# A short product ahead of the first projection, two buffers for the head products, and a new order of slots on all engines

## The chip, the cores and the metric

The kernel runs on one core of a Trainium2 chip. The metric is the time of one execution on the device in microseconds (us), launch to end; lower is better. All data are 32-bit floats, but for small mask matrices in bf16. A 32-bit product shows in the trace as two matmul records.

## What is computed

A gated cross-attention block followed by a gated feed-forward block, on x of shape (32, 56, 128). The context has 1500 rows for each batch item, but the causal mask lets 56 queries see only its first 56 rows.

```python
def xattn(Q, K, V):                       # 16 heads of 64
    q, k, v = heads(Q @ Wq), heads(K @ Wk), heads(V @ Wv)
    attn = softmax(where(causal, q @ k.T / 8, -1e9))
    return merge(attn @ v) @ Wo
def ffn(x):
    h = rmsnorm(x, gamma1)
    q = h @ Wq + bq                        # each token: 16 heads of 8
    k, v = split((h @ Wdown + bdown) @ Wup + bup)
    att = softmax(einsum('bthd,btgd->bthg', q, k) / sqrt(8))   # heads against heads, inside one token
    x = x + einsum('bthg,btgd->bthd', att, v) @ Wo + bo
    h2 = rmsnorm(x, gamma2)
    gate = softmax(h2 @ Wg + bg)           # 8 experts, all of them computed
    return x + einsum('btd,edf,bte->btf', h2, We, gate)
x = x + tanh(g_xattn) * xattn(layernorm(x), ctx, ctx)
x = x + tanh(g_ffn) * ffn(layernorm(x))
```

## The kernel before, in words

The five engines each run one instruction queue, written out by hand; the order of the calls in each block is the order of execution, and semaphores join the queues. There is no planner.

The attention works in 16 steps t of two batch items (T = 112 tokens). The feed-forward works in 14 tiles f of 128 tokens, with the stages of three or four successive tiles side by side in a step: in the loops, `fa` is the tile that enters in step t, `fb` the one that entered a step earlier, `fc` two and `fd` three steps earlier. Tile 9 is fa in step 12, tile 10 in step 13, tile 11 in step 14, tile 12 in step 15; tile 13 enters behind the last step. Lines 1065 to 1117 are TensorE's loops, 519 to 566 ScalarE's, 771 to 817 VectorE's, 359 to 384 GpSimd's; each engine has one loop for t = 2 to 13, one for t = 14 and 15, and then a list written out for the end, for tiles `third` = 11, `prior` = 12, `last` = 13. Steps 2 to 13 also hold the projection of queries or keys for later steps (`project`, PROJECT_AT); steps 14 and 15 hold none.

On TensorE a step is: `scores(t)`, `new_y(t-1)` (output projection of the attention), `turn_o` (transposes the head outputs of tile fc), `shift(t)` (subtracts the row maxima in PSUM), `bias_o`, `new_o`, the projections, `turn_x2`, two `values`, `turn_probs(t)`, `gate_logits`, `first(fa)` (transposes the new residual and makes q, k, v of the tile), `attend(t)`, two `expert_half`. A warm-up product of the identity (line 850) runs before the first key projection.

VectorE (DVE): `score_max` (L610), `products` (L642: part of the products query x key, for heads against heads), `new_x1` (L628), `logits` (L647: a reduction of 2048 products a row), `new_x2` (L685), `prob_sums` (L615), `norm` (L619, L622), `shifted_logits`, `weighted` (L661, L665), `gate_logits` (L691), `head_sums` (L674, again 2048 a row), `gate_sum`, `scaled_qkv` (L633), `head_scales` (L669), `normed_heads` (L680). GpSimd (POOL) makes the other heads' share of both kinds of product (L310, L318) and normalizes most of the probabilities (L300), sums the experts (L324 to L332), and does powers (L338, L342) and the gate (L347). ScalarE (ACT) copies PSUM out, takes exponentials (L430, L458, L478), `kv_copy` (L454: copies keys and values of the tile into PSUM, from where DVE's products read them), `squares` (L469, L470), `x2_copy` (L474) and the eight `experts` copies (L485).

`prod1` (query x key) and `prod2` (weight x value) are one buffer each, 8 KB a partition. Whoever writes a tile's products waits until the sums of the tile before are made. For tile 12 alone (PE_SUMS) TensorE makes both sums, by products with the identity (L994, L1001), and for tiles 10 to 12 (PE_OUT) it also adds the ten terms of the output (`output_sums`), which ScalarE copies out (`late_out`). The tail is what follows step 15: the serial chain of tiles 11, 12 and 13.

Of the kernel before, what the change touches and what calls it, by code (L numbers as in the profile page):

```python
# [14 lines left out]
D = 128  # L15
NP = 16
# [7 lines left out]
FH = 16  # L24
FD = 8
E = 8
L = 64
HP = 10
HQ = 6
# [12 lines left out]
def product_heads(f):  # L42
    return (HP_LATE, HQ_LATE) if f >= LATE else (HP, HQ)

# [10 lines left out]
LATE = 10  # L55
HP_LATE = 8
HQ_LATE = 5
PE_SUMS = (12,)
# [43 lines left out]
def build(nc, xp, x_t, ctx_t, wq, wk, wv, wo, fw, fup, fdn, fwe, out):  # L102
    with ExitStack() as stack:
# [66 lines left out]
        prod1 = sb("prod1", [128, FH, FH, FD])  # L170
        prod2 = sb("prod2", [128, FH, FD, FH])
# [42 lines left out]
        prod1_d = prod1[:, :, :, :].rearrange("p a b c -> p (a b c)").rearrange("p (d h g) -> p d h g", d=FD, h=FH)  # L214
        prod2_g = prod2[:, :, :, :].rearrange("p a b c -> p (a b c)").rearrange("p (g h d) -> p g h d", g=FH, h=FH)

        def logit_products(f, lo, hi, k, q):
            n = hi - lo
            if f in PE_SUMS:
                return (prod1_d[:, :, lo:hi, :],  # L220
                        k.rearrange("p (g d) -> p d g", g=FH).unsqueeze(2).to_broadcast([128, FD, n, FH]),
                        q.rearrange("p (h d) -> p d h", h=n).unsqueeze(3).to_broadcast([128, FD, n, FH]))
            return (prod1[:, lo:hi, :, :],
# [3 lines left out]
        def head_products(f, lo, hi, v):  # L227
            n = hi - lo
            if f in PE_SUMS:
                return (prod2_g[:, :, lo:hi, :],  # L230
                        e_sb[f % 2][:, lo:hi, :].rearrange("p h g -> p g h").unsqueeze(3).to_broadcast([128, FH, n, FD]),
                        v.rearrange("p (d g) -> p g d", d=FD).unsqueeze(2).to_broadcast([128, FH, n, FD]))
            return (prod2[:, lo:hi, :, :],
# [38 lines left out]
        def _(pool):  # L272
# [39 lines left out]
            def weighted(f):  # L312
                pool.wait_ge(s["e_ready"], f + 1)
                if f > 0:
                    pool.wait_ge(s["oraw_ready"], f)
# [84 lines left out]
        def _(act):  # L400
# [118 lines left out]
            for t in range(2, TAIL):  # L519
# [7 lines left out]
                if fc is not None:  # L527
                    squares(fc)
                    x2_copy(fc)
# [658 lines left out]
```

## Time and profile before

| | before |
|---|---|
| median of 3 runs | 265.05 us (264.35 to 265.61) |
| the profiled execution | 265.27 us, span 263.3 us |
| VectorE, ScalarE, GpSimd busy | 73%, 65%, 57% of the span |
| chain that ended last, by engine | PE 60%, DVE 17%, POOL 8%, issue 7%, ACT 5% |
| DMA, mean over the span | 28 GB/s, nearly all of it in the first tenth |

The span runs from the first to the last instruction of the profiled execution. Busy time is an average over stages with different limits: what an edit is worth is read where it lies, from what TensorE and the others wait for there.

### The profile page before, as it was taken

How to read it: one execution, taken by the hardware profiler on the slowest of the kernel's cores; microseconds unless marked ns; L12 is line 12 of the kernel's file. 1: busy time of each engine (PE TensorE's matmuls, PEld its weight loads, DVE VectorE, ACT ScalarE, POOL GpSimd, SP SyncE). 2: the span in 40 equal slices, each digit the busy share in tenths (PEclk: the TensorE clock that was granted, in tenths of full speed). 3: DMA queues.
4: the chain of work that ended last, by engine and by line, in shares of the span. 5: the costliest groups of instructions: out<-in, count | busy, mean ns of one | idle time of the engine just before them, and what ended most of it. 6: DMA issues, size and time to landing. Idle time of an engine off the chain costs nothing.

```text
span 263.3 us, 7886 instructions
## 1 busy us (share of the span) xinstructions
PE 246.5 (94%) x3242; PEld 177.4 (67%) x3242; DVE 192.0 (73%) x333; ACT 170.8 (65%) x501; POOL 149.8 (57%) x157
## 2 busy tenths in 40 slices
PE   5989989997989999999999999999899999988995
PEld 2775778675858676777678585867586656467664
DVE  0136744088989888898989751889898799968944
ACT  2437534756586877787787768675778676852273
POOL 4103030346468788787878473864796879656220
PEclk9999999999999999999999999999999999999999
DMA  6990000000000000000000000000000000000000
GB/s 211 365 311 9 2 4 0 5 1 2 2 2 0 12 4 10 4 10 5 11 2 12 2 11 2 0 15 0 2 2 10 4 14 4 10 2 0 10 2 30
DMA packets 6017, 7.30 MB, mean 28 GB/s; under 512 B 477, under 2 KB 4830, under 8 KB 5982
## 3 DMA queue, kind: packets, MB, share of 16 engines
q1 hardware_dynamic: 5550, 6.16, 7.3%
q8 instruction: 26, 0.43, 0.7%
q10 hardware_dynamic: 432, 0.64, 0.7%
q14 instruction: 9, 0.07, 0.1%
HBM read 5.88 MB, written 0.92 MB: 26 GB/s over the span
## 4 chain that ended last, share of the span: by engine, by line
PE 60%; DVE 17%; POOL 8%; issue 7%; ACT 5%; DMA 1%; POOLq 0%; SPq 0%; DVEq 0%
PE ps_a L853 34%; PE ps_c L853 9%; PE ps_b L853 7%; PE ps_e L853 6%; POOL prod L310 4%; PE ps_b L905 4%; DVE ps_e L674 3%; DVE ps_e L647 3%; POOL prod L318 2%; DVE psums L615 2%; DMA cT<-in_ctx_t 1%; DVE prod L665 1%; ACT probs L430 1%; POOL probs L300 1%; DVE fqkv L633 1%
## 5 line engine op out<-in xcount | busy, mean ns | idle before, releaser
L300 POOL TENSOR_TENSOR probs<-probs,prinv 120x672 f32<-120x672 f32 x16 | 24.3, 1517 | 38.5 <-DVE prinv L619 38.4
L310 POOL TENSOR_TENSOR prod<-fqkv 128x1280 f32<-128x1280 f32 (+1 forms) x14 | 38.7, 2762 | 5.5 <-DVE fqkv L633 2.7
L853 PE MATMUL ps_a<-aT,wo_sb 128*128 128x112 f32 x256 | 32.8, 281 | 0.6 <-ACT aT L424 0.3
L853 PEld LDWEIGHTS ps_a<-aT,wo_sb 128*128 128x128 f32 x256 | 29.9, 191 | 3.3 <-ACT aT L424 1.5
L853 PE MATMUL ps_a<-wv_sb,cT 128*64 128x512 f32 x128 | 31.4, 606 | 0.0
L647 DVE TENSOR_REDUCE ps_e<-prod 128x256 f32<-128x2048 f32 x13 | 29.7, 2285 | 1.8 <-POOL prod L310 1.8
L674 DVE TENSOR_REDUCE ps_e<-prod 128x128 f32<-128x2048 f32 x13 | 29.7, 2287 | 1.7 <-POOL prod L318 1.6
L853 PE MATMUL ps_a<-cT,wk_sb 128*128 128x224 f32 x128 | 29.4, 384 | 1.4 <-DMA cT<-in_ctx_t 1.4
L485 ACT ACTIVATE exb<-ps_c,gate 128x128 f32<-128x128 f32 x88 | 25.0, 386 | 6.2 <-POOL gate L347 6.2
L853 PEld LDWEIGHTS ps_a<-cT,wk_sb 128*128 128x128 f32 x128 | 24.9, 206 | 5.9 <-DMA cT<-in_ctx_t 3.0
L318 POOL TENSOR_TENSOR prod<-e_sb,fqkv 128x768 f32<-128x768 f32 (+1 forms) x14 | 24.5, 1752 | 6.2 <-PE ps_e L853 3.6
L853 PE MATMUL ps_a<-xT,wqc 128*128 128x224 f32 x128 | 27.0, 359 | 0.6 <-ACT qT L413 0.6
L413 ACT COPY kT<-ps_a 128x448 f32<-128x448 f32 x32 | 17.0, 532 | 13.7 <-PE ps_a L853 13.4
L610 DVE TENSOR_REDUCE nmax<-ps_b 120x16 bf16<-120x896 f32 x15 | 16.3, 1089 | 12.5 <-PE ps_b L853 12.5
L853 PEld LDWEIGHTS ps_a<-xT,wqc 128*128 128x128 f32 x128 | 22.7, 190 | 3.9 <-ACT qT L413 2.4
L853 PEld LDWEIGHTS ps_a<-probsT,v_sb 56*64 56x64 f32 x1024 | 16.5, 134 | 9.3 <-issue 5.7
L413 ACT COPY qT<-ps_a 128x448 f32<-128x448 f32 x32 | 16.9, 533 | 8.8 <-PE ps_a L853 8.7
L853 PE MATMUL ps_c<-fwe_sb,x2T 128*128 128x512 f32 x44 | 22.4, 623 | 0.1
L905 PEld LDWEIGHTS ps_b<-ident,probs 120*128 120x128 f32 x120 | 12.2, 140 | 14.7 <-issue 14.7
L419 ACT COPY v_sb<-ps_a 128x512 f32<-128x512 f32 x32 | 17.9, 589 | 5.4 <-PE ps_a L853 5.4
L665 DVE TENSOR_TENSOR prod<-e_sb,ps_e 128x1280 f32<-128x1280 f32 (+1 forms) x14 | 21.2, 1515 | 0.0
L430 ACT ACTIVATE probs<-ps_b,rstd 120x896 f32<-120x896 f32 x15 | 15.1, 1008 | 8.5 <-PE ps_b L853 7.5
(144 smaller groups left out, 487.7 us busy)
## 6 DMA issues: line engine op xcount, KB each, us to landing
xp_sb<-in_xp SPq DMA_DIRECT2D x1, 896.0 KB, 7.9
out<-out_sb SPq DMA_DIRECT2D x14, 64.0 KB, 1.5
xT<-in_x_t SPq DMA_DIRECT2D x1, 784.0 KB, 9.1
cT<-in_ctx_t SPq DMA_DIRECT2D x1, 784.0 KB, 10.7
wv_sb<-in_wv SPq DMA_DIRECT2D x1, 512.0 KB, 7.6
wo_sb<-in_wo SPq DMA_DIRECT2D x1, 512.0 KB, 12.3
fwe_sb<-in_fwe SPq DMA_DIRECT2D x1, 512.0 KB, 8.9
fw_sb<-in_fw SPq DMA_DIRECT2D x1, 266.0 KB, 12.2
```

Source lines behind the costliest of these rows:

```text
L300: nc.gpsimd.tensor_tensor(pr[0:TG, NC:C, :, 0:S], pr[0:TG, NC:C, :, 0:S], prinv[p % 2][0:TG, NC:C, :].unsqueeze(3).to_broadcast([TG, C - N ...
L310: nc.gpsimd.tensor_tensor(o, k, q, ALU.mult).then_inc(s["prod1_pool"], 1)
L318: nc.gpsimd.tensor_tensor(o, e, v, ALU.mult).then_inc(s["prod2_pool"], 1)
L413: nc.scalar.copy(dst[:, 2 * k:2 * k + 2, :], ps_a[:, b, 0:2 * GT].rearrange("p (c t) -> p c t", c=2)).then_inc(a_free[b], 1)
L419: nc.scalar.copy(v_sb[p % 2][:, bt, :, :], ps_a[:, b, :].rearrange("p (c d) -> p c d", c=C)).then_inc(a_free[b], 1)
L430: nc.scalar.activation(probs[p % 2][0:TG, :, :, 0:S].rearrange("p c r k -> p r c k"), score_banks(p)[0:TG, :, 0:C * S].rearrange("p r (c k ...
L485: last = nc.scalar.activation(exb[f % XB][:, e, :], expert_banks(f)[:, half, e % 4 * D:(e % 4 + 1) * D], ACT.Copy, scale=gate[f % 2][:, e: ...
L647: nc.vector.tensor_reduce(ps_e[:, f % 2, 0:2 * D].rearrange("p (h g) -> p h g", h=FH), prod1[:, :, :, :], AX.X, ALU.add).then_inc(s["logit ...
L665: nc.vector.tensor_tensor(o, e, v, ALU.mult).then_inc(s["prod2_ready"], 1)
L674: nc.vector.tensor_reduce(ps_e[:, f % 2, 0:D].rearrange("p (h d) -> p h d", h=FH), prod2[:, :, :, :], AX.X, ALU.add).then_inc(s["oraw_read ...
L853: return nc.tensor.matmul(o, lhsT, rhs, start=start, stop=stop, skip_group_check=True)
L905: ins = nc.tensor.transpose(score_banks(p)[:, ch // 4, ch % 4 * 128:ch % 4 * 128 + TG], probs[p % 2][0:TG, ch, :, :].rearrange("p r k -> p ...
```

## The change

It does four things.

1. The warm-up of one product of 512 columns becomes two, of 512 and of 384 columns.
2. `prod1` and `prod2` get two buffers each, by the tile's parity, so that writers wait for the sums of the tile two before. The count of sums becomes a function (`sums_made`), and the heads that TensorE sums a table (`LOGITS_BY_PE`, `HEADS_BY_PE`); their values, 16 heads for tile 12, keep the split as it was. So does POOL_HEADS (8 and 5 heads for tiles 10 to 13).
3. Steps 2 to 13: ScalarE has `x2_copy` ahead of `squares`, the first `attended` ahead of `gate_exps`, `kv_copy` ahead of the experts; DVE has `head_scales` right behind `weighted`; TensorE makes the second expert half first.
4. Steps 14 and 15 and the tail get a new order on TensorE, ScalarE, DVE and GpSimd.

```diff
-PE_SUMS = (12,)
+LOGITS_BY_PE = {12: 16}
+HEADS_BY_PE = {12: 16}
...
-        prod1 = sb("prod1", [128, FH, FH, FD])
-        prod2 = sb("prod2", [128, FH, FD, FH])
+        prod1 = two("prod1", [128, FH * FH * FD])
+        prod2 = two("prod2", [128, FH * FD * FH])
...
             def products(f):                                    # GpSimd; weighted(f) likewise
                 pool.wait_ge(s["qkv_ready"], f + 1)
-                if f > 0:
-                    pool.wait_ge(s["logit_ready"], f)
+                if f >= 2:
+                    pool.wait_ge(s["logit_ready"], sums_made(LOGITS_BY_PE, f - 2))
...
@@ GpSimd, steps 14 and 15, then the tail
                 outputs(fd)
+                second_scale(fc)
                 norm(t)
-                second_scale(fc)
...
             products(prior)
             first_scale(last)
+            second_scale(third)
             products(last)
             weighted(prior)
-            second_scale(third)
+            gating(third)
             weighted(last)
-            gating(third)
             second_scale(prior)
+            gating(prior)
             last_residual(last)
-            gating(prior)
             second_scale(last)
@@ ScalarE, steps 2 to 13
                 if fc is not None:
+                    x2_copy(fc)
                     squares(fc)
-                    x2_copy(fc)
...
+                if t < NP:
+                    attended(t, 0)
                 if fc is not None:
                     gate_exps(fc)
                 if t < NP:
-                    attended(t, 0)
                     attended(t, 1)
-                if fc is not None:
-                    experts(fc, 0)
                 if fa is not None:
                     kv_copy(fa)
                 if fc is not None:
+                    experts(fc, 0)
                     experts(fc, 1)
@@ ScalarE, steps 14 and 15
                 exps(t)
+                squares(fc)
+                values(t, 0)
                 x2_copy(fc)
-                values(t, 0)
-                squares(fc)
                 x1_copy(fa)
+                head_exps(fb)
                 values(t, 1)
+                gate_exps(fc)
                 turned_probs(t)
-                gate_exps(fc)
-                head_exps(fb)
+                kv_copy(fa)
                 attended(t, 0)
                 attended(t, 1)
-                kv_copy(fa)
+                experts(fc, 0)
                 experts(fc, 1)
-                experts(fc, 0)
@@ DVE, steps 14 and 15
+                products(fb)
                 score_max(t)
-                products(fb)
+                logits(fb)
                 new_x1(t - 1)
                 new_x2(fc)
                 prob_sums(t)
                 norm(t)
-                logits(fb)
+                shifted_logits(fb)
                 gate_logits(fc)
-                shifted_logits(fb)
+                weighted(fb)
                 scaled_qkv(fa)
                 gate_sum(fc)
-                weighted(fb)
                 head_scales(fb)
                 head_sums(fb)
@@ TensorE, the warm-up
-            nc.tensor.matmul(ps_b[:, 0, :], ident[:, :], ident[:, :].unsqueeze(1).to_broadcast([128, 4, 128]), start=True, stop=True)
+            for n in (4, 3):
+                nc.tensor.matmul(ps_b[:, 0, 0:n * 128], ident[:, :], ident[:, :].unsqueeze(1).to_broadcast([128, n, 128]), start=True, stop=True)
@@ TensorE, steps 14 and 15
                 shift(t)
+                values(t, 0)
                 bias_o(fc)
                 new_o(fc)
-                values(t, 0)
                 turn_x2(fc)
                 first(fa)
+                gate_logits(fc)
                 values(t, 1)
-                gate_logits(fc)
                 turn_probs(t)
```

The lists of the tail, as they stand after the change:

```python
# TensorE: last, prior, third = 13, 12, 11
new_y(15); turn_o(third); bias_o(third); new_o(third); first(last); logit_sums(prior)
output_sums(10); turn_x2(third); gate_logits(third); expert_half(third, 0); head_sums(prior)
expert_half(third, 1); turn_o(prior); bias_o(prior); new_o(prior); turn_x2(prior)
output_sums(third); gate_logits(prior); turn_o(last); bias_o(last); new_o(last)
expert_half(prior, 1); turn_x2(last); expert_half(prior, 0); gate_logits(last)
expert_half(last, 1); expert_half(last, 0); output_sums(prior)
# ScalarE
o_copy(third); x1_copy(last); squares(third); kv_copy(last); head_exps(prior); x2_copy(third)
gate_exps(third); head_exps(last); experts(third, 0); o_copy(prior); experts(third, 1)
squares(prior); x2_copy(prior); o_copy(last); late_out(10); late_out(third); gate_exps(prior)
squares(last); x2_copy(last); experts(prior, 1); experts(prior, 0); gate_exps(last)
experts(last, 0); late_out(prior)
# DVE, up to where it is as before
products(prior); new_x1(15); new_x2(third); scaled_qkv(last); shifted_logits(prior)
products(last); weighted(prior); gate_logits(third); head_scales(prior); logits(last)
shifted_logits(last); gate_sum(third); normed_heads(prior); weighted(last); new_x2(prior)
head_scales(last); head_sums(last); normed_heads(last)
```

## Rows read from the trace of the kernel before

**Rows 1.** The page: TensorE's share of busy time, its granted clock in 40 slices.
```profile
PE 246.5 (94%) x3242; PEld 177.4 (67%) x3242; DVE 192.0 (73%) x333; ACT 170.8 (65%) x501; POOL 149.8 (57%) x157
...
PEclk9999999999999999999999999999999999999999
```

**Rows 2.** Timeline of TensorE from the start: start us, length us, engine, line, operation.
```profile
1.56 2.08 PE L850 MATMUL ps_b<-ident 128*128 128x512 f32 x2 [1.56 <-POOL ident L276]
5.02 5.87 PE L853 MATMUL ps_a<-cT,wk_sb 128*128 128x224 f32 x16 [1.39 <-DMA cT<-in_ctx_t]
10.73 1.88 PE L853 MATMUL ps_e<-wq_sb,cmat 128*128 128x512 f32 x4
```

**Rows 3.** Timeline of ScalarE: its copies behind the key and the query projection.
```profile
8.42 0.53 ACT L413 COPY kT<-ps_a 128x448 f32<-128x448 f32 x1 [0.96 <-PE ps_a L853]
9.91 0.53 ACT L413 COPY kT<-ps_a 128x448 f32<-128x448 f32 x1 [0.96 <-PE ps_a L853]
10.93 0.53 ACT L413 COPY kT<-ps_a 128x448 f32<-128x448 f32 x1 [0.49 <-PE ps_a L853]
...
13.51 0.53 ACT L413 COPY qT<-ps_a 128x448 f32<-128x448 f32 x1 [1.13 <-PE ps_a L853]
14.26 0.53 ACT L413 COPY qT<-ps_a 128x448 f32<-128x448 f32 x1 [0.22 <-PE ps_a L853]
```

**Rows 4.** The query weights: the issue in the timeline, and the landing by DMA.
```profile
1.64 0.46 ACTq L403 DMA_DIRECT2D wq_sb<-in_wq  x1
...
wq_sb<-in_wq ACTq DMA_DIRECT2D x1, 256.0 KB, 4.9
```

**Rows 5.** Stretches: length; busy of PE, PEld, DVE, ACT, POOL; clock; DMA share; GB/s.
```profile
104.00:118.00 14.00, 14.00 (x199) 10.06 (x197) 12.45 (x20) 11.03 (x35) 10.99 (x12) 1.00 0.02 6
```

**Rows 6.** Timeline of all engines, step 14.
```profile
205.62 2.36 POOL L310 TENSOR_TENSOR prod<-fqkv 128x1024 f32<-128x1024 f32 x1
...
206.52 0.40 ACT L454 COPY ps_e<-fqkv 128x256 f32<-128x256 f32 x1
...
206.76 1.09 DVE L610 TENSOR_REDUCE nmax<-ps_b 120x16 bf16<-120x896 f32 x1 [0.67 <-PE ps_b L853]
207.77 1.21 DVE L642 TENSOR_TENSOR prod<-ps_e,fqkv 128x1024 f32<-128x1024 f32 x1
...
209.64 0.35 DVE L685 SCALAR_TENSOR_TENSOR x<-xc,rstd,ps_c 128x128 f32<-128x128 f32 x1 [0.42 <-PE ps_c L853]
...
210.22 1.09 DVE L615 TENSOR_REDUCE psums<-probs 120x16 f32<-120x896 f32 x1 [0.23 <-ACT probs L430]
...
211.67 1.52 POOL L300 TENSOR_TENSOR probs<-probs,prinv 120x672 f32<-120x672 f32 x1
...
211.94 2.29 DVE L647 TENSOR_REDUCE ps_e<-prod 128x256 f32<-128x2048 f32 x1
...
213.34 1.01 PE L905 MATMUL ps_b<-ident,probs 120*128 120x120 f32 x8 [0.38 <-POOL probs L300]
```

**Rows 7.** Timeline: the last output projection of the attention, behind step 15.
```profile
230.60 2.04 PE L853 MATMUL ps_a<-aT,wo_sb 128*128 128x112 f32 x16
```

**Rows 8.** Timeline of all engines in the tail, in order of time.
```profile
238.66 2.37 POOL L310 TENSOR_TENSOR prod<-fqkv 128x1024 f32<-128x1024 f32 x1 [1.79 <-PE ps_e L853]
...
242.85 3.81 PE L853 MATMUL ps_e<-prod,ident 128*128 128x128 f32 x32 [0.30 <-POOL prod L318]
...
253.07 0.35 DVE L685 SCALAR_TENSOR_TENSOR x<-xc,rstd,ps_c 128x128 f32<-128x128 f32 x1 [0.94 <-PE ps_c L853]
...
253.84 2.40 PE L853 MATMUL ps_e<-exb,ident 128*128 128x128 f32 x20
...
255.29 2.18 ACT L485 ACTIVATE exb<-ps_a,gate 128x128 f32<-128x128 f32 x8 [0.74 <-POOL gate L347]
...
256.07 0.29 PE L853 MATMUL ps_c<-fwg_sb,x2T 128*128 128x8 f32 x2
...
257.30 0.32 ACT L478 ACTIVATE ps_c<-glog,gmax 128x8 f32<-128x8 f32 x1
```

More of the change, by code:

```diff
@@ L42, in product_heads, with sums_made @@
 def product_heads(f):
-    return (HP_LATE, HQ_LATE) if f >= LATE else (HP, HQ)
+    return POOL_HEADS.get(f, (HP, HQ))
+def sums_made(by_pe, f):
+    return sum((by_pe.get(n, 0) > 0) + (by_pe.get(n, 0) < FH) for n in range(f + 1))
 def first_step(f):
@@ L212, in expert_banks, with logit_tiles, head_tiles @@
             return {"a": ps_a, "b": ps_b}[BIG[f]] if f in BIG else ps_c
[L214 to L215 removed]
+        def logit_tiles(f):
+            n, t = LOGITS_BY_PE.get(f, 0), prod1[f % 2]
+            return (t[:, 0:n * FH * FD].rearrange("p (d h g) -> p d h g", d=FD, h=n) if n else None,
+                    t[:, n * FH * FD:].rearrange("p (h g d) -> p h g d", g=FH, d=FD) if n < FH else None)
+        def head_tiles(f):
+            n, t = HEADS_BY_PE.get(f, 0), prod2[f % 2]
+            return (t[:, 0:n * FH * FD].rearrange("p (g h d) -> p g h d", g=FH, h=n) if n else None,
+                    t[:, n * FH * FD:].rearrange("p (h d g) -> p h d g", d=FD, g=FH) if n < FH else None)
         def logit_products(f, lo, hi, k, q):
[L218 to L220 removed]
+            n, by_pe, (tp, td) = hi - lo, LOGITS_BY_PE.get(f, 0), logit_tiles(f)
+            if hi <= by_pe:
+                return (tp[:, :, lo:hi, :],
                         k.rearrange("p (g d) -> p d g", g=FH).unsqueeze(2).to_broadcast([128, FD, n, FH]),
                         q.rearrange("p (h d) -> p d h", h=n).unsqueeze(3).to_broadcast([128, FD, n, FH]))
[L223 removed]
+            return (td[:, lo - by_pe:hi - by_pe, :, :],
                     k.rearrange("p (g d) -> p g d", g=FH).unsqueeze(1).to_broadcast([128, n, FH, FD]),
@@ L553, in _ @@
                 exps(t)
+                squares(fc)
+                values(t, 0)
                 x2_copy(fc)
-                values(t, 0)
-                squares(fc)
                 x1_copy(fa)
+                head_exps(fb)
                 values(t, 1)
+                gate_exps(fc)
                 turned_probs(t)
-                gate_exps(fc)
-                head_exps(fb)
+                kv_copy(fa)
                 attended(t, 0)
                 attended(t, 1)
-                kv_copy(fa)
+                experts(fc, 0)
                 experts(fc, 1)
-                experts(fc, 0)
             last, prior, third = NT - 1, NT - 2, NT - 3
+            o_copy(third)
             x1_copy(last)
-            o_copy(third)
+            squares(third)
+            kv_copy(last)
             head_exps(prior)
-            kv_copy(last)
-            squares(third)
             x2_copy(third)
+            gate_exps(third)
             head_exps(last)
-            late_out(PE_OUT[0])
-            o_copy(prior)
-            gate_exps(third)
-            x2_copy(prior)
-            squares(prior)
-            experts(third, 1)
-            o_copy(last)
-            experts(third, 0)
+            experts(third, 0)
+            o_copy(prior)
+            experts(third, 1)
+            squares(prior)
+            x2_copy(prior)
+            o_copy(last)
+            late_out(PE_OUT[0])
+            late_out(third)
             gate_exps(prior)
@@ L589, in _ @@
             gate_exps(last)
-            late_out(third)
             experts(last, 0)
@@ L819, in _ @@
             last, prior, third = NT - 1, NT - 2, NT - 3
+            products(prior)
             new_x1(NP - 1)
-            products(prior)
+            new_x2(third)
             scaled_qkv(last)
             shifted_logits(prior)
-            new_x2(third)
+            products(last)
             weighted(prior)
-            products(last)
+            gate_logits(third)
             head_scales(prior)
@@ L829, in _ @@
             shifted_logits(last)
-            gate_logits(third)
+            gate_sum(third)
             normed_heads(prior)
@@ L834, in _ @@
             head_scales(last)
-            gate_sum(third)
             head_sums(last)
@@ L1120, in _ @@
             new_y(NP - 1)
+            turn_o(third)
             bias_o(third)
+            new_o(third)
             first(last)
             logit_sums(prior)
-            turn_o(third)
-            new_o(third)
             output_sums(PE_OUT[0])
@@ L1128, in _ @@
             gate_logits(third)
+            expert_half(third, 0)
             head_sums(prior)
+            expert_half(third, 1)
+            turn_o(prior)
             bias_o(prior)
-            turn_o(prior)
             new_o(prior)
-            expert_half(third, 1)
             turn_x2(prior)
-            expert_half(third, 0)
+            output_sums(third)
             gate_logits(prior)
-            expert_half(prior, 0)
             turn_o(last)
@@ L1142, in _ @@
             turn_x2(last)
-            output_sums(third)
+            expert_half(prior, 0)
             gate_logits(last)
```

56 lines of the change are left out of this document (31 added, 25 removed).

## Prediction

> **What bounds the kernel now.** I read the page's shares first, then the engine's own waits, then the timeline where those waits lie. TensorE (PE) is busy for 94% of the span [rows 1], and in the middle of the run (one step per two batch items) the table of stretches shows it busy without a hole, VectorE (DVE) and GpSimd (POOL) having air [rows 5]. A new order of the other engines' work is worth nothing there, as long as it makes nobody later than TensorE. So the change can only act where TensorE waits or runs slowly: the first 12 us, the two last attention steps, and the 31 us behind them, where the last three feed-forward tiles pass serially over all engines.
>
> The start: the granted clock reads 9 tenths from the first slice on [rows 1], but the durations disagree. ScalarE's copies behind the key projection follow each other by 1.49 us for four matmul records, those behind the query projection by 0.75 us [rows 3]. The same records take exactly twice as long: 1.2 GHz against 2.4 GHz. Between the third and the fourth key copy lie 1.02 us; with 0.373 a record slow and 0.187 fast, 1.02 = 0.373n + 0.187(4 - n) gives n = 1.5, so the clock rose at 5.02 + 13.5 x 0.373 = 10.05 us, 5.0 us after the projections began. The product on the identity that runs before them, 1.56 to 3.64, is followed by 1.4 us of idleness [rows 2] and brought nothing.
>
> **The warm-up.** One product of 512 columns (two records, 2.08 us) becomes two, of 512 and 384. At the slow rate a record of 224 columns takes 0.373, so one of 512 takes 0.85 and one of 384 takes 0.64. Four records end at 1.56 + 2 x 0.85 + 2 x 0.64 + 0.2 of drain = 4.75 us, before the keys' input lands at 5.02: nothing is queued behind them that could have run earlier, with 0.27 us to spare; if the input came at once, they would cost that much. TensorE is then occupied from 1.56 with a hole of only 0.27 us instead of 1.4. Before, the rise came 5.0 us after unbroken work began; counted from 1.56 it falls at 6.6. Then 4.2 records run slowly and 9.2 records that were slow run fast, at 0.19 saved each: **-1.7 us**. The bounds: nothing (the hole counts as a new start) and -2.5 (fast from 5.02 on: 13.5 x 0.187). I take 1.7, since it moves a measured distance. Next behind it are transfers: the weights of the queries, issued at 1.64, landed 4.9 later at 6.5 [rows 4]; they were used at 10.73 [rows 2] and would be at 9.0. The rest of the front is a chain of TensorE, ScalarE and DVE, which moves as a whole.
>
> The Trainium skill ("TensorE: Matmul & The Clock Gate", Part 1) says that the low level is the default which activity releases, and that the moment differs from run to run. It also says the ramp costs under 1% of a typical span: an estimate by that sentence caps this term at 2.6 us, just above my -2.5. Its statement on runs makes my 1.7 a mean that single runs miss; that is the first rival below.
>
> **Steps 2 to 13.** On ScalarE the copy of x2T goes ahead of the squares, and the copy of the feed-forward keys and values (kv_copy) ahead of the eight expert copies; one DVE reciprocal comes forward, the expert halves change places. Each exchange moves a result by one or two instructions of 0.2 to 1 us under a TensorE that is full [rows 5]: 0, bounds -0.2 and +0.2 over all. The double buffers of the head products bring nothing here either: POOL's products wait for this tile's qkv, which comes long after the previous tile's sums.
>
> **Steps 14 and 15.** Here DVE gets a new order: products of the heads before the score maximum, and the long reduction (logits, 2.29 us) before new_x1, new_x2 and the sums of the probabilities, on which POOL's normalization and TensorE's transposes hang. Step 14 walked along, in the times of before: qkv is there at about 205.6, when POOL's products start. kv_copy no longer waits for four expert copies and starts then instead of at 206.52; DVE's products run 206.05 to 207.2 (1.21, overlapping the next), the maximum to 208.2 (score products end at 206.7), the reduction needs POOL's products, which end at 205.62 + 2.36 = 207.98, and takes DVE to 210.4; x1 and x2 at about 0.3 each, and the sums start at 210.9 against 210.22. POOL's normalization moves by the same, 211.67 to 212.33, ends at 213.85, and the transposes go from 213.34 to 213.98, **+0.64** [rows 6]. TensorE gives part of it back: the expert product now follows the transposes with its input ready, where it had waited for the gate logits, so the step ends +0.4. In exchange the reduction after the normalization (211.94) is gone, and the tile's output is 1.2 us earlier in front of step 15. There DVE starts its queue 1.2 us sooner, pays 2.2 for the reduction and ends at +0.8 at the transposes, +0.55 at the last attention output (before: 230.60 [rows 7]). Bounds: 0 and +4.4, two whole reductions.
>
> **The tail.** The +0.55 is mostly swallowed at once: TensorE's logit sums of tile 12 had waited for DVE's product and not for TensorE's own queue, and the walk has them beginning only 0.1 later. From there on: (1) POOL's products of tile 13 start at 238.66, 1.79 after they could, because the one buffer was being summed [rows 8]. With two buffers their qkv decides, 237.9. So POOL's second product of tile 12 ends 0.7 earlier, and the head sums on TensorE, at 242.85 before, start when DVE is done, 242.55: **-0.3**. This -0.3 persists through the second reduction to tile 13's x2, 253.07 to 252.8. (2) The output sums of tile 11 (20 records, 2.4 us) stood between the transposition of tile 13's x2 and its gate logits, 253.84 to 256.07. They move ahead, into the wait for tile 13's head output. What is late next? The row scale r2, which needs squares (0.5), POOL's residual and power (0.5 each): 254.9, and ScalarE, which after x2T has the eight expert copies of tile 12 before tile 13's gate exponentials. They take 257.30 - 255.29 = 2.0 us. They had waited for a gate at 255.29; the new order has gate and products ready when ScalarE finishes x2T, at 252.8 + 1.2 = 254.0. The gate exponentials then start at 254.0 + 2.05 = 256.05 instead of 257.30: **-1.25**, the -0.3 included. From there to the end everything is as before, 6.0 us. Bounds: -0.3 (the sums merely change places with another wait) and -2.2 (all of the 2.4 us, less what the next engine adds).
>
> **The sum.** 265.27 (the profiled execution; its span 263.3 and 2.0 around it) - 1.7 - 1.25 = 262.3. That execution lies 0.2 above the median 265.05, so the prediction is **262.1**, with 261.2 to 263.0 as the likeliest case's own range (0.3 for the clock, 0.5 for the walk).
>
> **The rivals.**
> - The warm-up moves nothing: the clock keeps its own schedule or takes the hole for a new start. For it: 2.08 us of activity in front brought nothing so far, and the hole remains. Against it: the hole shrinks from 1.4 to 0.27. Time 265.05 - 1.25 = 263.8. Chance 0.12. By the Trainium skill's sentence on differences from run to run (same page, Part 1) it would be so in some executions only; no trace here shows more than one start.
> - The tail gives its gain back: the moved output sums now stand before tile 13's transposition of the head output (my walk has 0.2 us between them), or ScalarE's late copies push the exponentials. Then 265.05 - 1.7 - 0.3 = 263.1. Chance 0.13.
> - Both gain more: an early rise (-2.5) and DVE in steps 14 and 15 covered by TensorE: 260.7. Chance 0.08.
> - Slower: the long reduction ahead of the probability sums. If DVE's earlier start does not absorb it, each of steps 14 and 15 is 2.2 longer, 4.4 in place of the 0.55 of my walk: 262.1 + 3.85 = 266.0. The kernel is slower than before once the two steps lose more than 0.55 + 2.95 = 3.5 together. For it: in step 14 only 0.2 us lie between POOL's last product (207.98) and DVE's readiness (208.2), so every delay of POOL passes on [rows 6]. Against it: kv_copy is 0.9 earlier, and in step 15 the room is 2 us. Chance 0.07, a little over half of it past the 266.4 that would count as slower.
> - My forecast: 0.60.
>
> **How the numbers follow.** About 0.5%, 1.3 us, can be told from no change here, so faster means under 263.7. That is all of the forecast and of the third rival, and most of the second: 0.60 + 0.08 + 0.09 = 0.77. Same takes the first rival (0.12) and the rest of the second and the fourth (0.04 and 0.03): 0.19. Slower 0.04. The range goes from 260.7 to 263.9, which leaves out the slower case, and the edges of the others.
>
> **What would show it.** Key copies on ScalarE 0.75 us apart from the second or third on, and the query weights' product at about 9.0 instead of 10.73; nothing waits for a transfer. Steps of 14.1 us in the middle as before. In step 14 the transposes 0.6 us later against the start of the step, the reduction before the sums. In the tail, POOL's products of tile 13 begin before TensorE's logit sums end; the gate exponentials of the last tile 24.9 us after the last attention output projection begins, against 26.7 before (257.30 - 230.60). Wrong would be: the fourth key copy still 1.0 us or more after the third with the product at 10.7; new holes of over 1 us in steps 14 and 15 whose releaser is x2; or the last gate logits again waiting on TensorE.

## The result, and the profile after

The changed kernel takes 262.34 us (median of 4 runs, 260.77 to 262.57); the kernel before took 265.31 on the same chip (264.35 to 265.61). The ratio is 0.9882, with an interval of 0.9835 to 0.9928. In a later set of runs it was 261.74 against 265.05, 0.9885 (0.9866 to 0.9904). Predicted were 262.1, 260.7 to 263.9. The profiled execution took 262.38, with a span of 260.3; that of before had 263.3.

The page, answering to [rows 1]: busy times, the granted clock, and the chain that ended last by engine.

```profile
PE 245.8 (94%) x3244; PEld 177.2 (68%) x3244; DVE 190.3 (73%) x333; ACT 171.4 (66%) x501; POOL 150.1 (58%) x157
...
PEclk9999999999999999999999999999999999999999
...
PE 67%; DVE 19%; POOL 6%; ACT 6%; issue 2%; DVEq 0%; POOLq 0%; ACTq 0%
```

Busy times moved by under 2 us each. In the chain the share of "issue" went from 7% to 2%, but that is no measure of the gain: it would be 13 us, and another execution of the same changed kernel (a_again, below) has 4%. Where the 3.0 us lie has to be read from the timelines. First TensorE's start, answering to [rows 2], and ScalarE's key copies, answering to [rows 3].

```profile
1.56 3.35 PE L868 MATMUL ps_b<-ident 128*128 128x512 f32 x4 [1.56 <-POOL ident L289]
4.93 4.67 PE L871 MATMUL ps_a<-cT,wk_sb 128*128 128x224 f32 x16
9.44 1.88 PE L871 MATMUL ps_e<-wq_sb,cmat 128*128 128x512 f32 x4
```

```profile
6.83 0.53 ACT L426 COPY kT<-ps_a 128x448 f32<-128x448 f32 x1 [3.22 <-PE ps_a L871]
8.00 0.53 ACT L426 COPY kT<-ps_a 128x448 f32<-128x448 f32 x1 [0.63 <-PE ps_a L871]
8.76 0.53 ACT L426 COPY kT<-ps_a 128x448 f32<-128x448 f32 x1 [0.23 <-PE ps_a L871]
```

The warm-up ends at 4.91 and the projection follows at 4.93, without the hole. The first two copies are 1.17 apart and the next two 0.76: by the equation of the prediction 1.17 is 2.3 slow records and 1.7 fast ones, so the clock rose at 4.93 + 6.3 x 0.373 = 7.3 (predicted 6.6, before 10.05). The query weights' product starts at 9.44 (predicted 9.0, before 10.73).

The last 20 us, answering to [rows 8], first on TensorE.

```profile
245.98 0.39 PE L871 MATMUL ps_c<-fw_sb,ident 128*128 128x128 f32 x2
246.75 0.49 PE L871 MATMUL ps_c<-fw_sb,oT 128*128 128x128 f32 x2 [0.39 <-ACT oT L476]
247.68 0.33 PE L984 MATMUL ps_c<-ident,x 128*128 128x128 f32 x1 [0.44 <-DVE x L702]
247.85 2.47 PE L871 MATMUL ps_e<-exb,ident 128*128 128x128 f32 x20
250.15 0.29 PE L871 MATMUL ps_c<-fwg_sb,x2T 128*128 128x8 f32 x2
250.32 0.33 PE L967 MATMUL ps_c<-ident,onorm 128*128 128x128 f32 x1
...
252.20 0.27 PE L984 MATMUL ps_c<-ident,x 128*128 128x128 f32 x1
...
253.17 0.28 PE L871 MATMUL ps_c<-fwg_sb,x2T 128*128 128x8 f32 x2
```

The output sums (20 records, 2.47 us) now run between the transpositions of tile 12's x2 and tile 13's head output, where TensorE would wait. Behind the transposition of tile 13's x2 (252.20) the gate logits come 0.97 later; before, with the sums in between, it was 2.34 (253.73 to 256.07). Next, ScalarE's and DVE's last instructions: gate exponentials and last output.

```profile
252.67 2.18 ACT L498 ACTIVATE exb<-ps_a,gate 128x128 f32<-128x128 f32 x8
254.68 0.33 ACT L491 ACTIVATE ps_c<-glog,gmax 128x8 f32<-128x8 f32 x1
...
257.54 0.27 ACT L505 COPY out_sb<-ps_e 128x128 f32<-128x128 f32 x1 [0.71 <-PE ps_e L871]
```

```profile
258.00 0.29 DVE L743 TENSOR_TENSOR out_sb<-exb 128x128 f32<-128x128 f32 x1
```

The exponentials start when ScalarE is through the eight expert copies, 24.55 us after the last attention output projection (230.13); before it was 26.70.

All runs below are read in the same segments. The columns: the start of the query weights' product; the length of step 14, from its first score products to those of step 15, and of step 15, from there to the last output projection; from the last output projection to the gate exponentials of tile 13; from those to the end of the span; the span. The times stand beside before on the same chip. Left out of the ratios are one execution of e4_no_hole (347.46 us, mean granted clock 0.659; it is its only trace, so it has no row here) and one of before (348.51 us).

| run | product | step 14 | step 15 | to the exponentials | to the end | span | median | before | ratio (interval) |
|---|---|---|---|---|---|---|---|---|---|
| before | 10.73 | 12.13 | 13.00 | 26.70 | 6.00 | 263.3 | | | |
| changed | 9.44 | 12.68 | 13.03 | 24.55 | 5.62 | 260.3 | 262.34 | 265.31 | 0.9882 (0.9835, 0.9928) |
| a_again, the same | 8.86 | 12.68 | 13.31 | 24.56 | 5.67 | 259.8 | 261.74 | 265.05 | 0.9885 (0.9866, 0.9904) |
| e1_warm_only | 8.34 | 12.12 | 13.00 | 26.68 | 6.03 | 260.9 | 263.15 | 264.87 | 0.9947 (0.9927, 0.9967) |
| e2_no_warm | 10.20 | 12.67 | 13.02 | 24.54 | 5.62 | 260.8 | 262.65 | 264.87 | 0.9925 (0.9904, 0.9947) |
| e3_no_product | 9.77 | 12.12 | 12.99 | 26.70 | 5.99 | 261.9 | 264.40 | 264.87 | 0.9988 (0.9971, 1.0004) |
| e5_one_buffer | 8.25 | 12.67 | 13.02 | 24.89 | 5.66 | 259.8 | 261.87 | 264.73 | 0.9902 (0.9874, 0.9930) |
| e6_two_buffers | 10.36 | 12.13 | 12.99 | 26.48 | 7.60 | 264.3 | 265.21 | 264.73 | 1.0018 (0.9997, 1.0039) |
| e7_old_steps | 8.87 | 12.12 | 13.00 | 25.91 | 5.62 | 260.5 | 262.39 | 264.73 | 0.9920 (0.9893, 0.9947) |
| e8_sums_late | 9.43 | 12.68 | 13.23 | 28.80 | 6.37 | 265.2 | 265.95 | 264.73 | 1.0059 (1.0030, 1.0088) |
| e9_filler | 8.53 | 12.68 | 13.02 | 26.06 | 6.36 | 261.9 | 264.47 | 265.05 | 0.9982 (0.9958, 1.0007) |
| e11_split | 8.75 | 12.13 | 14.68 | 24.56 | 5.66 | 260.5 | 262.75 | 265.05 | 0.9932 (0.9903, 0.9962) |
| e12_split_early | 8.39 | 12.13 | 14.69 | 24.55 | 5.64 | 260.6 | 262.94 | 265.05 | 0.9939 (0.9917, 0.9962) |

What the table leaves out hardly differs: from the product to the scores of step 2 28.62 us (29.22 in e5_one_buffer), steps 3 to 13 154.2 in all. Only step 2 has between 11.48 and 12.42, mostly by a pause of TensorE in its output projection, of at most 0.70 us (0.42 in the changed kernel, 0.20 before), for which the profile names no releaser ("issue"), and which goes with no edit (step 2 took 12.15 and 11.88 in two executions of the changed kernel). Such pauses, of 0.60 and 0.52 us, also stand in step 15 of a_again (13.31) and e8_sums_late (13.23). So the change's 3.0 us of span are: front -1.29, step 2 +0.22, steps 14 and 15 +0.58, up to the exponentials -2.15, from there to the end -0.38.

### The profile page after: what moved, and what is told of

Read it like the earlier page. It is cut to its first block, busy times and chain, and to the rows that moved or that the text cites. A ratio compares the mean times of both kernels' runs of the same rounds, so it can differ in the third digit from the quotient of the medians.

```text
span 260.3 us, 7887 instructions
## 1 busy us (share of the span) xinstructions
PE 245.8 (94%) x3244; PEld 177.2 (68%) x3244; DVE 190.3 (73%) x333; ACT 171.4 (66%) x501; POOL 150.1 (58%) x157
## 4 chain that ended last, share of the span: by engine, by line
PE 67%; DVE 19%; POOL 6%; ACT 6%; issue 2%; DVEq 0%; POOLq 0%; ACTq 0%
PE ps_a L871 35%; PE ps_c L871 10%; PE ps_e L871 7%; PE ps_b L871 7%; DVE ps_e L662 4%; PE ps_b L923 4%; POOL prod L323 3%; DVE ps_e L691 2%; DVE psums L628 2%; DVE prod L680 2%; POOL probs L313 2%; ACT exb L498 2%; PE ps_b L868 1%; DVE fqkv L646 1%; DVE nmax L623 1%
## 5 line engine op out<-in xcount | busy, mean ns | idle before, releaser
L871 PE MATMUL ps_a<-cT,wk_sb 128*128 128x224 f32 x128 | 28.2, 372 | 0.0
L871 PEld LDWEIGHTS ps_a<-cT,wk_sb 128*128 128x128 f32 x128 | 23.7, 198 | 4.0 <-ACT kT L426 1.9
L498 ACT ACTIVATE exb<-ps_c,gate 128x128 f32<-128x128 f32 x88 | 23.9, 381 | 1.1 <-POOL gate L360 0.8
L437 ACT COPY aT<-ps_a 128x448 f32<-128x448 f32 x32 | 16.3, 531 | 6.2 <-PE ps_a L871 6.0
## 6 DMA issues: line engine op xcount, KB each, us to landing
fw_sb<-in_fw SPq DMA_DIRECT2D x1, 266.0 KB, 11.9
```

The lines of the kernel that those rows point to most:

```text
L498: last = nc.scalar.activation(exb[f % XB][:, e, :], expert_banks(f)[:, half, e % 4 * D:(e % 4 + 1) * D], ACT.Copy, scale=gate[f % 2][:, e: ...
L871: return nc.tensor.matmul(o, lhsT, rhs, start=start, stop=stop, skip_group_check=True)
```

## The experiments

**The warm-up by itself, and the rest by itself.** e1_warm_only is the kernel before with this edit alone; e2_no_warm the changed kernel with the opposite edit.

```diff
-            nc.tensor.matmul(ps_b[:, 0, :], ident[:, :], ident[:, :].unsqueeze(1).to_broadcast([128, 4, 128]), start=True, stop=True)
+            for n in (4, 3):
+                nc.tensor.matmul(ps_b[:, 0, 0:n * 128], ident[:, :], ident[:, :].unsqueeze(1).to_broadcast([128, n, 128]), start=True, stop=True)
```

> The kernel before with only the two warm-up products (512 and 384 columns) in place of one. Theory (the rise of TensorE's clock moves forward with the start of nearly unbroken work): the product of the query weights starts near 9.4 us as in the changed kernel, 1.3 us earlier than before, all later stages keep their lengths, and the time is 1.3 us below the kernel before, 264.0. Rival (the clock keeps its own schedule and the changed kernel's trace was one lucky phase): the product starts near 10.7 and the time is that of before, 265.3.

> The changed kernel with the single old warm-up product. Theory: the front returns to the old one (query weights near 10.7), everything behind keeps the changed lengths, 262.3 + 1.3 = 263.6, so 1.7 below the kernel before by the new order alone. Rival (the new order brought it all, the clock nothing on the mean): 262.3.

The ratio 0.9947 on 264.87 is -1.4 us (0.9 to 1.9); 0.9925 is -2.0 (1.4 to 2.5). The two make 3.4 together, within their intervals the -3.05 of the same kernel in a_again. Both parts gain; by these figures the new order gains more, though the two intervals overlap. Expected were 1.3 and 1.7. e1_warm_only's start on TensorE:

```profile
1.56 3.31 PE L851 MATMUL ps_b<-ident 128*128 128x512 f32 x4 [1.56 <-POOL ident L276]
5.02 3.49 PE L854 MATMUL ps_a<-cT,wk_sb 128*128 128x224 f32 x16
```

The same 16 records took 5.87 us before [rows 2], 4.67 in the changed kernel and 3.49 here, all fast from the first. So what the warm-up brings differs from one execution to the next.

**How little, and how much, warm-up.** e3_no_product is the kernel before without its product; e4_no_hole has `for n in (4, 3, 1)`, which ends behind the landing of the keys' input; e12_split_early (below) has products from a tile of ones that DVE writes first, `for n in (4, 4, 1)`, so that they begin at 1.04 and not at 1.56.

> The kernel before without any product ahead of the first projection (it is not part of the result). Theory (the old product, followed by 1.4 us of idleness, bought nothing): 265.3 and query weights near 10.7, as before. Rival (any activity in front helps a little): up to 0.8 us slower, the key copies 1.49 us apart up to the last one.

> The kernel before with three products ahead, of 512, 384 and 128 columns, so that they end at the moment the keys' input lands and the hole of some 0.1 to 0.3 us closes. Theory (the small hole costs nothing): as with two products, 264.0, query weights near 9.4. Rival (the hole still delays the rise): the rise comes earlier by up to 1.5 us and the time is 263.3 to 263.5. If the third product is in the way of the keys, they start up to 0.2 later.

Without any product the query weights' product starts at 9.77, and the ratio is 0.9988 (0.9971 to 1.0004): the one product of before was worth nothing that can be measured. e4_no_hole took 263.66 against 264.87, 0.9952 (0.9935 to 0.9968), like e1_warm_only: closing the last hole adds nothing that can be measured. Over the traces of the table, the one with three products (e12_split_early, 8.39) left out, with one product or none the start was at 10.73, 10.20, 10.36 and 9.77 (mean 10.27), with two at 9.44, 8.34, 8.25, 8.87, 9.43, 8.86, 8.53 and 8.75 (mean 8.81): **-1.46**, and the two groups do not overlap.

The moment of the rise moves between executions with the same first 5 us. The Trainium skill ("TensorE: Matmul & The Clock Gate", Part 1) says so too, and here the traces agree: the query weights' product starts at 8.86 and 9.44 in two executions of one and the same kernel.

**The buffers.** e5_one_buffer is the changed kernel with one buffer, e6_two_buffers the kernel before with two (and the waits of DVE for PE_SUMS dropped, which the second buffer makes needless).

```diff
-        prod1 = two("prod1", [128, FH * FH * FD])
-        prod2 = two("prod2", [128, FH * FD * FH])
+        prod1 = [sb("prod1", [128, FH * FH * FD])] * 2
+        prod2 = [sb("prod2", [128, FH * FD * FH])] * 2
...
-                if f >= 2:
-                    pool.wait_ge(s["logit_ready"], sums_made(LOGITS_BY_PE, f - 2))
+                if f >= 1:
+                    pool.wait_ge(s["logit_ready"], sums_made(LOGITS_BY_PE, f - 1))
```

> The changed kernel with one buffer again for each kind of head product, and the waits that go with it; all orders as changed. Theory (POOL's products of tile 13 then wait for TensorE's logit sums of tile 12, near 237.4 instead of 236.9, and the second kind for the head sums): 0.5 to 1.0 us slower than the changed kernel, 262.9 to 263.3. Rival (the buffers carry most of the tail's gain): 1.5 or more slower, 263.8 and above. Rival (the order carries all): 262.3.

> The kernel before with only the second buffers and their relaxed waits, no order changed, no longer warm-up. Theory (in the old order DVE's product and then TensorE's own queue follow): POOL's products of tile 13 start 0.8 earlier (near 237.9), the head sums 0.2 to 0.3 earlier, the last gate logits remain behind the output sums: 265.1, within 0.3 of before. Rival (the buffers are the gain of the tail): 1 us or more below before, under 264.3.

POOL's products of tile 13 in e5_one_buffer:

```profile
236.65 2.36 POOL L323 TENSOR_TENSOR prod<-fqkv 128x1024 f32<-128x1024 f32 x1 [0.84 <-PE ps_e L871]
```

They wait 0.84 for TensorE's sums; in the changed kernel they wait for qkv alone (236.89, 0.20). The exponentials come 24.89 after the last output projection and not 24.55: the buffers are worth 0.34 in the new order and 0.22 in the old (26.70 against 26.48). Neither can be seen in a time: 0.9902 has 0.9885 in its interval, and 1.0018 has 1. For e5_one_buffer I had expected a loss of 0.5 to 1.0, which was too much, and 262.9 to 263.3, which its early front (product at 8.25) put further off; the segment is what answers the question. The profiled execution of e6_two_buffers ends 1.6 later than that of before, counted from the exponentials: its last two output transfers landed 3.4 and 3.2 us after their issue, against 1.5 and 1.6 before. Why they did stays open.

**The order of steps 14 and 15.** e7_old_steps is the changed kernel with the loops `for t in range(TAIL, END)` of before on all four engines; warm-up, buffers and the lists of the tail stay new.

> The changed kernel with the old order in steps 14 and 15 on all four engines; warm-up, buffers and the new tail stay. Theory (the new order costs 0.55 in the two steps, and the tail swallows most of it): the last attention output starts 0.55 earlier than in the changed kernel, the tail is longer by as much, 262.3 within 0.3. Rival (what the steps lose is lost): 261.8. Rival (the new order of the steps is what makes the new tail fast, by earlier outputs of tile 11): 263 or more.

The steps are back at 12.12 and 13.00, 0.59 less, but the tail takes 25.91 instead of 24.55. DVE around the last output projection (228.97 in this run), e7_old_steps:

```profile
229.15 2.25 DVE L691 TENSOR_REDUCE ps_e<-prod 128x128 f32<-128x2048 f32 x1
231.43 0.29 DVE L697 TENSOR_TENSOR onorm<-ps_e,einv 128x128 f32<-128x128 f32 x1
231.64 1.21 DVE L655 TENSOR_TENSOR prod<-ps_e,fqkv 128x1024 f32<-128x1024 f32 x1
232.77 0.32 DVE L641 SCALAR_TENSOR_TENSOR x1T<-ps_a,gates,xT 128x112 f32<-128x112 f32 x1
```

The changed kernel (projection at 230.13):

```profile
228.66 2.23 DVE L691 TENSOR_REDUCE ps_e<-prod 128x128 f32<-128x2048 f32 x1
230.93 0.29 DVE L697 TENSOR_TENSOR onorm<-ps_e,einv 128x128 f32<-128x128 f32 x1
231.14 1.22 DVE L655 TENSOR_TENSOR prod<-ps_e,fqkv 128x1024 f32<-128x1024 f32 x1
```

With the reduction of the logits made early in the step, DVE comes to the head output of tile 11 (`onorm`) 0.80 after the projection's start, against 2.46 in e7_old_steps, and TensorE's logit sums of tile 12 begin 3.63 after it and not 4.99. In e7_old_steps, in the changed kernel and in the kernel before:

```profile
233.96 3.62 PE L871 MATMUL ps_e<-prod,ident 128*128 128x256 f32 x16
```

```profile
233.76 3.62 PE L871 MATMUL ps_e<-prod,ident 128*128 128x256 f32 x16
```

```profile
234.79 3.72 PE L853 MATMUL ps_e<-prod,ident 128*128 128x256 f32 x16 [0.15 <-DVE prod L642]
```

That is all of the 1.36: from these sums to the exponentials both kernels take 20.9. So in front of the new lists the order of the two steps costs 0.59 and gives 1.36 behind: **-0.77** net. The times agree in size (0.9920 against 0.9885, 0.9 us), though their intervals overlap. The median, 262.39, is the one that the theory had expected, but the segments show what the second rival said: the early outputs of tile 11 are what makes the new tail fast.

Against the kernel before, the steps' gain is smaller. There the sums begin 4.19 after the projection, since in its lists `first(last)` waits neither on TensorE for `turn_o(third)`, which needs that head output, nor on DVE for `products(prior)`, which now stands ahead of `new_x1`. So the new lists lose 0.80 at this place if the steps stay old, and with the new steps 0.56 is gained. The steps and the lists belong together; no run has the new steps in front of the old lists. Behind the sums the lists and buffers bring 1.59 (22.51 before, 20.92 in the changed kernel); with one buffer in place of two 0.34 of it is lost (e5_one_buffer, 21.26).

**The place of the output sums.** e8_sums_late moves them back behind tile 13's x2, in the changed kernel; `late_out(third)` goes behind `gate_exps(last)` on ScalarE.

```diff
             turn_x2(prior)
-            output_sums(third)
...
             expert_half(prior, 0)
+            output_sums(third)
             gate_logits(last)
```

> The changed kernel with TensorE's output sums of tile 11, and ScalarE's copy of them, back at their old place between the last transposition of x2 and the last gate logits. Theory (this one move is the main gain of the tail): the last gate logits start about 2 us later, the last gate exponentials about 1.0 to 1.3 later, 263.3 to 263.6. Rival (something else is late next anyway): 262.3 to 262.6.

The exponentials came 4.25 later and not 1.0 to 1.3. A move of 2.4 us of work does not explain that. TensorE in stretches (start:end, length, busy time and records, granted clock, DMA share, GB/s), e8_sums_late:

```profile
245.00:250.00 5.00, 2.47 (x11) 0.96 0.00 0
250.00:255.00 5.00, 4.78 (x10) 0.50 0.04 13
255.00:259.00 4.00, 4.00 (x25) 0.82 0.01 4
```

The changed kernel:

```profile
245.00:250.00 5.00, 4.17 (x29) 1.00 0.00 0
250.00:255.00 5.00, 4.89 (x21) 1.00 0.10 30
```

Once the sums are gone from 247.85, TensorE is busy for 2.47 of 5 us, and the granted clock falls to 0.50, which is 1.2 GHz. The unprofiled executions have it too: the mean granted clock is 0.987 to 0.994 in all eight, against 0.998 to 1.000 in the changed kernel. TensorE's timeline of e8_sums_late shows what came before and what it costs:

```profile
250.22 0.47 PE L967 MATMUL ps_c<-ident,onorm 128*128 128x128 f32 x1 [1.38 <-DVE onorm L697]
...
251.64 1.92 PE L871 MATMUL ps_a<-fwe_sb,x2T 128*128 128x512 f32 x2
```

The expert half of 1.03 us takes 1.92. The Trainium skill ("TensorE: Matmul & The Clock Gate", "Why this matters for your kernels") names long idle gaps between bursts as what loses the clock, longer ones than any here: the longest was 1.38 us, with several of 0.4 to 0.6 ahead of it. Here these shorter ones were enough, and the measurement decides.

To part the two effects, e9_filler is e8_sums_late with three products of the identity, of no use otherwise, where the sums had been:

```diff
             gate_logits(prior)
+            for n in range(3):
+                mm(ps_c[:, 0, 256:512], ident[:, :], ident[:, :].unsqueeze(1).to_broadcast([128, 2, 128]))
             turn_o(last)
```

> The changed kernel with the output sums of tile 11 late, as in the run before of that kind, but with three products on the identity (256 columns each, into an unused stretch of PSUM, read by nobody) in the 1.4 us in which TensorE then waits for tile 13's head outputs. Theory (of the 4.2 us that the late place cost up to the last gate exponentials, over half came from the granted clock falling to the lower level while TensorE stood idle): the clock stays up, the last gate exponentials lie 25.6 to 26.2 us after the last attention output instead of 28.8, time 263.3 to 264. Rival (the clock falls in any case, or its fall costs little): 28 or more, time above 265.

```profile
245.00:250.00 5.00, 3.63 (x17) 1.00 0.00 0
250.00:255.00 5.00, 4.94 (x33) 1.00 0.05 16
```

With 1.54 us of filler the clock stays, and the exponentials come at 26.06: in these traces the place of the sums is worth 1.5 us, the clock 2.74. The trace of e8_sums_late is the longest of its eight executions (267.27, median 265.95), so 2.74 is a high value. The median, 264.47, is above what I expected, since the filler holds the clock in only half of the ten runs: five have a mean granted clock of 0.999 and lie at 262.99 to 263.97, five have 0.992 to 0.994 and lie at 264.98 to 265.82, 1.8 us apart by their medians.

The kernel before has its sums late too and did not lose the clock (0.998 to 1.000 in the executions of the table's ratios); TensorE has more to do there in the same window:

```profile
245.00:250.00 5.00, 4.42 (x25) 1.00 0.04 13
250.00:255.00 5.00, 4.51 (x24) 1.00 0.00 0
```

So none of the 3.0 us of the whole change comes from the clock in the tail. From the logit sums of tile 12 to the exponentials e9_filler takes 22.43, the kernel before 22.51 and the changed kernel 20.92: but for 0.08, what is gained there goes with the place of the sums.

**The same kernel again, and an attempt at both gains.** If step 14's +0.55 could be saved and the gain behind step 15 kept, the kernel would be faster still. e11_split has the old order in step 14 and the new in step 15; e12_split_early has the earlier warm-up as well.

> The changed kernel once more, on the chip of the two that follow, so that they can be held against it. Expected: the same lengths from the last attention output to the last gate exponentials (24.5 us) as in its first trace, steps 14 and 15 of 12.7 and 13.0 us, and the product of the query weights anywhere from 8.2 to 9.5 us, since that has moved between 8.25 and 9.44 in the kernels with two warm-up products. Ratio to before 0.988 within 0.003.

> The changed kernel with the old order in step 14 and the new one in step 15. Theory (the 0.55 that step 14 costs is the DVE reduction ahead of the probability sums; what speeds the tail is step 15's order alone): step 14 takes 12.1 us, step 15 13.0 to 13.2, the tail 24.5 to 24.6, so 0.4 to 0.5 below the changed kernel. Rival (step 15 needs the early head outputs of step 14 for its new order): step 15 takes 13.6 or more, no gain.

> The same split, and the warm-up on a tile that DVE fills as its first instruction, so that it starts near 1.05 us instead of 1.56, with products of 512, 512 and 128 columns (the tile is no part of the result). Theory (the rise moves with the start of unbroken work): 0.2 to 0.3 below the split alone on the mean. Rival (the landing of the query weights, up to 9.6 us in one run, is the bound of the front now): no difference from the split alone.

Step 14 is back at 12.13 and the tail at 24.56, but step 15 takes 14.68. TensorE in step 15 of e11_split:

```profile
218.61 0.27 PE L1013 MATMUL ps_c<-ident,onorm 128*128 128x128 f32 x1
220.61 0.59 PE L917 MATMUL ps_b<-nmax,ident_b 120*120 120x448 bf16 x2 [1.72 <-DVE nmax L651]
```

TensorE waits 1.72 us for the row maxima. The new order of step 15 has DVE's products ahead of the maximum, and DVE, behind the two reductions that the old order leaves at the end of step 14, comes to these products 2.74 after the step's first score products (218.34 - 215.60); in the changed kernel it is 1.08 (218.18 - 217.10). The two orders work only as a pair. The medians are 262.75 and 262.94 against 261.74 for the changed kernel on the same chip; the earlier warm-up (keys fast from 5.06, product at 8.39) shows in no time either. In each of the two, three of twelve executions have a mean granted clock of 0.986 to 0.993 and take 263.98 to 265.63; without them the medians would be 262.49 and 262.88, still above 261.74. So the clock was lost at times although the sums stood early; where, no trace shows. No version tried beat the changed kernel.

## Why the prediction was right

The time was 0.2 us from the forecast, the gain 3.0 where 2.95 was said. That closeness is in part luck: in the profiled execution the front and step 2 gave 1.07 where 1.7 was said, and all from step 14 on gave 1.95 where 1.25 was said. The mechanisms held. By its steps:

- **The warm-up, -1.7.** Right in mechanism and mis-sized: -1.29 in the first trace, -1.46 over the traces, -1.4 (0.9 to 1.9) in time. What failed is "I take 1.7, since it moves a measured distance": the distance from the start of the work to the rise is not fixed. The clock rose at 7.3 in the changed kernel, at or before 5.0 in e1_warm_only and e5_one_buffer, at 10.05 before. The bounds (0 and -2.5) hold all of them. The hole of 0.27 that one rival feared cost nothing that can be measured (e4_no_hole).
- **"Nothing waits for a transfer"** held in the profiled run, not always. The query weights landed 4.9 us after their issue before [rows 4], 5.9 in the changed kernel, 8.0 in e5_one_buffer, where TensorE waited:

```profile
8.25 1.02 PE L871 MATMUL ps_e<-wq_sb,cmat 128*128 128x512 f32 x2
9.71 1.12 PE L871 MATMUL ps_e<-wq_sb,cmat 128*128 128x512 f32 x2 [0.44 <-DMA wq_sb<-in_wq]
```

- **Steps 2 to 13, nothing.** Right: the scores of step 3 to those of step 14 take 154.2 us in every run of the table.
- **Steps 14 and 15, +0.4 and +0.15.** Measured +0.55 and +0.03, together +0.58 against +0.55. In step 14 the reduction stands where the walk had it, and the transposes follow:

```profile
204.42 0.38 PE L871 MATMUL ps_b<-hide_b,ident_b 56*64 56x448 bf16 x4
204.57 2.37 POOL L323 TENSOR_TENSOR prod<-fqkv 128x1024 f32<-128x1024 f32 x1
...
207.06 2.28 DVE L662 TENSOR_REDUCE ps_e<-prod 128x256 f32<-128x2048 f32 x1
...
210.04 1.08 DVE L628 TENSOR_REDUCE psums<-probs 120x16 f32<-120x896 f32 x1
...
213.15 1.01 PE L923 MATMUL ps_b<-ident,probs 120*128 120x120 f32 x8 [0.21 <-POOL probs L313]
```

  From the step's first score products to the transposes are 8.73 us, 7.87 before [rows 6]: +0.86 where +0.64 was said. The slower rival (a reduction of 2.28 not absorbed in each step) was wrong, as DVE's queue in step 15 does start early enough.
- **"The +0.55 is mostly swallowed at once".** Right: the two steps take 0.58 more, and the logit sums of tile 12 begin 0.56 sooner behind the projection, so 0.02 is left where the walk had 0.1. What it hangs on, which the walk does not name, is DVE's head output of tile 11, 1.66 earlier; without it the new lists start these sums 0.80 late (e7_old_steps against before).
- **The tail's lists and buffers, -1.25.** Right in mechanism, a little short: from the logit sums to the exponentials 1.59 is gained where the walk had 1.35.
- **Two buffers, -0.3.** Measured -0.34 in the new order, -0.22 in the old. The prediction reads the 1.79 of [rows 8] as POOL's wait for the buffer, but that is all of its idle time there, the wait for the tile's qkv included: with two buffers in the old order its products start 1.06 sooner behind the projection (e6_two_buffers, 7.00 after it and not 8.06), where "237.9" meant 0.8.
- **What comes after the moved sums.** Right: ScalarE's eight expert copies end last, and the exponentials follow them at once. Their place is worth 1.5 in the new order with the clock kept (e9_filler). Left late there, they would also have lost the clock, another 2.74 in the trace, which the prediction did not see.
- **"From there to the end everything is as before, 6.0 us".** Missed by 0.38. Before, ScalarE's last copy of tile 12 began at 260.55 and DVE's last output at 260.61; now 257.54 and 258.00. So the two last output transfers no longer come to SP's queue together. The last issue, before and in the changed kernel:

```profile
261.21 0.43 SPq L267 DMA_DIRECT2D out<-out_sb  x1
```

```profile
258.32 0.33 SPq L280 DMA_DIRECT2D out<-out_sb  x1
```

  Before, DVE's output ended at 260.90 and the issue came 0.31 later, behind that of ScalarE's copy (260.84); now it ends at 258.30 and the issue comes 0.02 later. The issue itself is 0.10 shorter. Together that is 0.39, the whole of what was missed, and all traces of the table fall into two groups: where the two issues follow each other at once (before, e1, e3, e6, e8, e9) the exponentials are 5.99 to 7.60 from the end, elsewhere 5.62 to 5.67.

The chance for "the warm-up moves nothing", 0.12, did not reckon with starts that spread by 1.2 us between executions (8.25 to 9.44), though none with two products fell back to those with one or none. In the fourth rival two figures do not fit: its time, 266.0, lies below the 266.4 past which "a little over half" of its chance is put. Nothing hung on it.

## What to carry to other kernels

Cost a new order on the engine that feeds the serial tail, not only on the one that is busiest: 0.59 us spent in two steps bought 1.36 behind them with the new lists, and half of the edit (e11_split) kept the gain but paid 1.1 us more in the steps. An ablation that takes one part out of a change prices that part in front of the others, not against the kernel before. Useful work moved into a wait of TensorE can gain twice when the stretch is thin, by its own length (1.5 us here) and by the clock it holds (2.74 in the traces of e8_sums_late and e9_filler), so look at the granted clock of the stretch that the work would leave. An order of 1 us and a clock start that moves by 1 us are told apart in segments of the trace, not in medians alone.

## What the runs showed of the hardware

- The granted clock of the profile reads 9 tenths or 1.00 in the first 10 us, where many records take twice their later time (in the kernel before, copies 1.49 us apart at first and 0.75 later, [rows 3]); the same figure does show the fall in the tail (0.50 at 250 to 255 in e8_sums_late). Durations decide at the start.
- The clock fell behind a thin stretch (2.47 us busy between 245 and 250) at the end of a run that had been over 90% busy; with 1.54 us of filler there it held in five of ten executions. In the kernel before, busy for 4.42 us of the same window, it held.
- The same transfer of 256 KB, issued in the same place, landed after 4.9 to 8.0 us. Transfers of 64 KB at the end, mostly 1.5 us from issue to landing, took 3.2 and 3.4 in e6_two_buffers.
